# Last two layers of a four-layer stack: keys ahead of the weights' product on POOL, squares ahead of the turned weights on DVE

## The reference

```python
def _layer(x, wqkv, qs, ksc, wo, lg, lb, w1, b1, w2, b2):
    h = shift_token(x)
    q, k, v = split(h @ wqkv)              # 8 heads of 64
    q = l2norm(q) * qs;  k = l2norm(k) * ksc
    q, k = rotary_xpos(q, k)
    o = local_attention(q, k, v)           # softmax over this window of 64 and the one before
    x = x + o @ wo
    ...                                    # layer norm, gated feed-forward
    return x
```

## Time and profile before

| what | us |
|---|---|
| median of 3 runs | 1707.55 (1704.67 to 1719.86) |
| the profiled execution | 1716.1 |
| its span, first to last instruction | 1714.3 |
| PE busy (share of the span) | 1424.1 (83%) |
| DVE busy | 1084.5 (63%) |
| ACT busy | 780.0 (45%) |
| POOL busy | 401.3 (23%) |

### The profile page before, as it was taken

How to read it: one execution, slowest core, us unless ns; L and a number is a source line. 1 busy time by engine, 2 the same in 40 slices (tenths; PEclk the granted TensorE clock), 3 DMA queues, 4 the chain that set the end, 5 groups by cost and what they waited for, 6 DMA issues and landing times.

```text
span 1714.3 us, 25564 instructions
## 1 busy us (share of the span) xinstructions
PE 1424.1 (83%) x9075; PEld 819.3 (48%) x9075; DVE 1084.5 (63%) x2293; ACT 780.0 (45%) x1648; POOL 401.3 (23%) x258
## 2 busy tenths in 40 slices
PE   6999999999999689954579999984588868788766
PEld 4777777777777433222013333222255543355542
DVE  6776766766767537675646666514767744677644
ACT  2444544544444133322035656553367743477731
POOL 2000000000000103342202130001478830578811
PEclk9999999999999789976569999888689988699978
DMA  5000000000000000012201111102000000000000
GB/s 124 1 1 1 0 0 0 0 0 0 0 0 0 1 1 0 0 49 99 75 36 60 66 65 65 57 2 56 1 1 0 1 1 1 1 0 0 1 1 25
DMA packets 26097, 33.82 MB, mean 20 GB/s; under 512 B 5970, under 2 KB 20508, under 8 KB 24732
## 3 DMA queue, kind: packets, MB, share of 16 engines
q1 hardware_dynamic: 26028, 32.91, 6.0%
HBM read 28.51 MB, written 4.39 MB: 19 GB/s over the span
## 4 chain that ended last, share of the span: by engine, by line
PE 62%; POOL 14%; DVE 8%; issue 7%; ACT 3%; DMA 3%; SPq 2%; POOLq 0%; DVEq 0%; ACTq 0%
PE ps L658 14%; PE ps L689 7%; PE ps L700 7%; POOL d_rn L1954 5%; PE ps L894 5%; PE ps L914 5%; PE ps L872 4%; POOL probsT L1965 4%; PE ps L823 2%; POOL k_st L1952 2%; POOL q_st L1952 2%; PE ps L817 2%; PE ps L645 2%; PE ps L810 2%; DVE stats L1120 1%
## 5 line engine op out<-in xcount | busy, mean ns | idle before, releaser
L1731 ACT ACTIVATE probsT<-ps 128x512 f32<-128x512 f32 (+1 forms) x304 | 166.2, 575 | 153.8 <-PE ps L898 137.1
L1221 DVE TENSOR_REDUCE negmax<-ps 128x1 f32<-128x1024 f32 x128 | 150.7, 1219 | 76.1 <-PE ps L689 76.1
L1631 ACT ACTIVATE probs<-ps,negmax 128x1024 f32<-128x1024 f32 x128 | 142.7, 1115 | 76.2 <-DVE negmax L1221 75.9
L1637 ACT COPY probsT<-ps 128x512 f32<-128x512 f32 x128 | 75.0, 586 | 177.8 <-PE ps L700 177.7
L894 PE MATMUL ps<-arena 79*128 79x512 bf16 (+3 forms) x384 | 116.9, 350 | 31.1 <-DMA arena<-c_maxima 23.4
L700 PEld LDWEIGHTS ps<-ident,probs 128*128 128x128 f32 x1024 | 114.7, 141 | 58.3 <-issue 53.5
L1389 DVE CUSTOM_DVE_ANT_0 xn<-ps,arena 128x128 f32<-128x128 f32 (+7 forms) x128 | 93.3, 756 | 77.6 <-PE ps L872 76.1
L700 PE MATMUL ps<-ident,probs 128*128 128x128 f32 x1024 | 136.3, 276 | 0.0
L658 PE MATMUL ps<-probsT,v_nat 128*128 128x256 f32 x554 | 129.9, 380 | 0.0
L1389 DVE CUSTOM_DVE_ANT_0 xn<-ps,probs 128x128 f32<-128x128 f32 (+7 forms) x128 | 93.5, 756 | 56.8 <-PE ps L872 55.7
L689 PE MATMUL ps<-k_st,q_st 64*128 64x512 f32 x512 | 127.2, 615 | 2.2 <-DVE v_st L1200 1.4
(11 more groups left out here) (255 smaller groups left out, 2743.2 us busy)
## 6 DMA issues: line engine op xcount, KB each, us to landing
arena<-c_parts SPq DMA_DIRECT2D x32, 192.0 KB
c_parts<-probsT SPq DMA_DIRECT2D x4, 768.0 KB, 4.4
yT<-c_parts SPq DMA_DIRECT2D x32, 96.0 KB
arena<-c_parts SPq DMA_DIRECT2D x16, 128.0 KB
arena<-in_L_ffn_w_dram SPq DMA_DIRECT2D x3, 512.0 KB
work<-in_L_ffn_wqkv_dram SPq DMA_DIRECT2D x1, 1536.0 KB
q_st<-c_parts SPq DMA_DIRECT2D x16, 96.0 KB
k_st<-c_parts SPq DMA_DIRECT2D x16, 96.0 KB
```

Source lines behind the costliest of these rows:

```text
L1221: dve.tensor_reduce(negmax[:, u:u + 1], s2, AX_X, ALU.max, negate=True)\
L1631: act.activation(probs[:, u % NPB, :], s2, ACT.Exp, bias=negmax[:, u:u + 1], accum_out=rowsum[:, u:u + 1]).then_inc(s_a_exp, 1)
L1731: act.activation(c_p[:, kt % 2, j0:j0 + heads, q0 - kt * P:q0 - kt * P + n], ps[:, 4 + c % 2, 0:heads * n].rearrange("p (h n) -> p h n", n ...
```

## The change

POOL does `unit_norm` of tile t+2 ahead of the weights' product of tile t. The power then no longer stands behind the exponentials of tile t, so two things guard `d_rn`: DVE copies the queries' half of it to a new tile `d_rq`, from which the exponentials take their scale, and POOL's power waits for DVE's row product of tile t (`s_d_nm8`), which stands behind that copy. On DVE, `norms` of tile t+2 moves ahead of the copy of the turned weights of tile t-1.

```diff
--- before.py
+++ after.py
@@ -269,6 +269,7 @@
         d_nm = sb("d_nm", [P, 2, H2])
         d_nm8 = sb("d_nm8", [P, 2, H2])
         d_rn = sb("d_rn", [P, 2, 2 * H2])
+        d_rq = sb("d_rq", [P, 2, H2])
         d_sum = sb("d_sum", [P, 2, H2])
         d_rr = sb("d_rr", [P, 2, H2])
         d_mA = probs[:, 0:2, :]
@@ -1513,17 +1514,18 @@
                         dve.wait_ge(s_d_s, n + 1)
                         dve.tensor_reduce(d_nm[:, par, :], ps[:, 6:8, :].rearrange("p n (h c) -> p (n h) c", c=P),
                                           AX_X, ALU.max).then_inc(s_d_nm, 1)
+                        dve.tensor_copy(d_rq[:, par, :], d_rn[:, par, 0:H2])
                         dve.wait_ge(s_d_nm, n + 1)
                         dve.scalar_tensor_tensor(out=d_nm8[:, par, :].rearrange("p (c m) -> p c m", c=2),
                                                  in0=d_nm[:, par, :].rearrange("p (c m) -> p c m", c=2), scalar=-1.0,
                                                  in1=d_rn[:, par, 0:H2].rearrange("p (m c) -> p c m", c=2),
                                                  op0=ALU.mult, op1=ALU.mult).then_inc(s_d_nm8, 1)
+                    if exists(t, 2):
+                        norms(t + 2, par)
                     if exists(t, -1):
                         dve.wait_ge(s_d_pt, n)
                         dve.tensor_copy(d_pT[:, 4:8, :].rearrange("p h c -> p (h c)"), ps[:, 5, :])\
                            .then_inc(s_d_pT, 1)
-                    if exists(t, 2):
-                        norms(t + 2, par)
                     if exists(t, -2):
 
                         dve.wait_ge(s_d_w, n - 1)
@@ -1799,7 +1801,7 @@
                             hd = 2 * (h % 4) + h // 4
                             ins = act.activation(d_p[:, par, h, :], ps[:, 6 + h // 4, (h % 4) * P:(h % 4 + 1) * P],
                                                  ACT.Exp, bias=d_nm8[:, par, h:h + 1],
-                                                 scale=d_rn[:, par, hd:hd + 1],
+                                                 scale=d_rq[:, par, hd:hd + 1],
                                                  accum_out=d_sum[:, par, h:h + 1])
                         ins.then_inc(s_d_e, 1)
                     if exists(t, -1):
@@ -1951,6 +1953,8 @@
                     pool.wait_ge(s_d_m, n + 1)
                     pool.tensor_tensor(kq, d_mA[:, par, :], d_mB[:, par, :], ALU.add).then_inc(s_d_add, 1)
                     pool.wait_ge(s_d_cl, n + 1)
+                    if exists(t, -2):
+                        pool.wait_ge(s_d_nm8, n - 1)
                     pool.tensor_tensor(d_rn[:, par, :], ss[:, par, :], half_c[:, :], ALU.pow).then_inc(s_d_rn, 1)
                     pool.wait_ge(s_d_add, n + 1)
                     pool.wait_ge(s_d_rn, n + 1)
@@ -1959,13 +1963,13 @@
                         .then_inc(s_d_kq, 1)
 
                 def step(t, par):
+                    if exists(t, 2):
+                        unit_norm(t + 2, par)
                     if exists(t, 0):
                         v = d_p[:, par, :, :]
                         pool.wait_ge(s_d_rr, T0 + t + 1)
                         pool.tensor_tensor(v, v, d_rr[:, par, :].unsqueeze(2).to_broadcast([P, H2, P]), ALU.mult)\
                             .then_inc(s_d_p, 1)
-                    if exists(t, 2):
-                        unit_norm(t + 2, par)
 
                 unit_norm(0, 0)
                 unit_norm(1, 1)
```

## The result

The changed kernel takes 1796.09 us as a median of 4 runs (1794.47 to 1809.08), beside 1710.10 (1704.67 to 1719.86, 4 runs) for the kernel before: slower, ratio 1.0513 with a 95% interval of 1.0443 to 1.0583, +86.0 us. Its profiled execution took 1796.78, with a span of 1795.0. A ratio is estimated from the fast runs on the same chip, so it need not be the quotient of the two medians.

A forecast was written before the change was run, and what follows sets the result against it. A loop of waits, not an engine, was taken to set the pace: 9.62 + 1.38 + 1.22 = 12.22, with 1.7 for the clock 13.92 us per tile; with the ends +85.6, median 1793 us, range 1735 to 1820.

The forecast's parts named there:

- those of +108: Rival: the clock falls at the larger price, 2.61 us, in every tile; 14.83 us per tile, 1815 us; chance 0.07.
- The ring: Loop of waits from DVE's turned-weights copy through PE, ACT and DVE's rotation back to that copy: 9.62 us per tile.
- the wait: DVE's copy to d_rq, ahead of the row product, has to wait for POOL's add of the keys: +1.22 us per tile.
- the squares: DVE's sum (1.21) and clamp (0.17) now stand ahead of the copy of the turned weights: +1.38 us per tile.
- the clock: PE idles 3.9 us before line 1059, its clock falls, transposes and projection slow: +1.7 us in every tile.
- the loop through the exponentials: ACT's own loop: 9.93 + 1.22 = 11.15 us per tile, staying below the 12.22 us sum.
- the upper bound: For DVE's copy to d_rq beside POOL's add: bounds 0 and 1.22 us per tile, of which 1.22 was taken.
- the smaller of the two prices: Slowing of PE's transposes and projection (2.68 us) seen in the warm-up: +1.67 us, against +2.61.
- The rival in which the clock holds: PE's clock does not fall in the steady steps: 12.22 us per tile, +45 us, 1752 us; chance 0.17.
- the ends: Each layer's end: last-keys wait goes (2.2 us), last weights come 2.7 later, +0.5 us; step 0 counted separately at 1.22.
- The one that let nobody wait: Neither DVE's copy nor its row product waits for POOL: 11.00 us per tile, 1721 us, or 1762; chance 0.10.
- The rival on the other side: POOL's keys decide if the turned-weights copy (line 1523) ends before PE finishes line 1045: 1695 us; chance 0.06.

The follow-up runs named there:

- Experiment 1: Changed kernel with PE's output product of line 1046 computed four times over into the same place: 1769.24 us, ratio 1.0352.
- experiment 2: Changed kernel with DVE's sum and clamp put back behind the copy of the turned weights: 1730.44 us, ratio 1.0120.
- experiments 4 and 5: Both against the changed kernel: without the copy to d_rq, power waiting for the exponentials, 1802.21 us; POOL's row-product wait moved from power to add, 1793.92 us.
- experiment 3: Kernel before with only DVE's sum and clamp moved ahead of the copy of the turned weights: 1741.46 us, ratio 1.0195.
- Experiment 6: Changed kernel with POOL's row-product wait moved up to the add, and sum and clamp back behind the turned weights: 1717.84 us, ratio 1.0016.
- experiment 7: Kernel before with PE's projection of tile t+2 ahead of tile t's transposes, ACT and DVE reordered to suit: 1695.45 us, ratio 0.9925.
- experiment 8: Kernel before with PE's projection first, plus DVE's copy of value rows moved behind its copy of inputs: 1694.29 us, ratio 0.9888.

## Why the prediction was right

It gave 1793 us, +85.6; measured were 1796.09, +86.0. Its steps by the rows above, in us from a rotation, predicted and then measured: row product 4.80 and 4.78; line 1059 (now 1060) 7.06 and 6.97; the weights' product done 12.6 and 12.4; PE's idle time 3.9 and 3.80; the copy 1.3 and 1.40, ending with the add; transposes 1.9 and 1.97; clock below 0.9 and 0.87. No transposes waited for POOL, and the clamp released POOL's power. Two of the prediction's sums are off by rounding, without effect: the terms of 7.06 add up to 7.05, and those of +108 to +107.

**The loop.** The ring that the prediction put at 9.62 now reads: rotation to maximum 2.34 as before; maximum to row product 2.44 in place of 1.24; to the copy of the turned weights 1.41 in place of 0.09; copy and the start behind it 0.78, as before; line 1060 to the transposes 1.37 in place of 1.17; transposes to projection 1.76 in place of 0.90; projection to rotation 3.58 in place of 3.10. That is 13.68. The first two growths, 1.20 and 1.32, are the wait and the squares (predicted 1.22 and 1.38); the last three, 0.20 + 0.86 + 0.48 = 1.54, are the clock. Experiment 1, which gives back the clock alone, agrees: 12.10 (predicted 12.22) and 1.59 (predicted 1.7). So all three terms were a little too large, and a tile came to 13.68 in place of 13.92: 12 tiles took 164.18 and 163.22 us, not 167.0. That the loop through the exponentials is the next longest, with 11.15, had no row of its own in the prediction; experiment 2, with 11.13, bears it out.

**The copy's wait.** The value taken, the upper bound, was right, and experiments 4 and 5 show why it made no difference which operation waits: the row product or the clamp would have waited nearly as long.

**The clock.** That it would fall in every tile was the riskiest step, and it fell at a little under the smaller of the two prices (projection 2.39, not 2.68). Across the kernels here, with 1.76 us of idling before the weighted values it held in the steady steps of experiment 2 (1.00 from 1271.44 to 1371.42), with 2.7 to 2.8 in experiment 3 it fell in about every second tile, and with 3.8 in the changed kernel in each. The idle time ahead of that one line does not decide alone, since in the warm-up it fell with less. The rival in which the clock holds was wrong only in this; experiment 1 has its step, 12.10 us for 12.22, though not its 1752 us, since the added products lengthen the ends. The one that let nobody wait fell with the copy's 1.40.

**The term that was mis-sized** is the ends. The layer's end was put at +0.5 and measured 37.03 in place of 34.65 and 37.19 in place of 35.19, +2.4 and +2.0; step 0 was put at +1.22 and measured +1.29 and +1.95 (11.33 in place of 10.04 and 9.38). The clock had been charged to the 12 steady steps only. Behind the last rotation of layer 0, PE's timeline of the kernel after shows

```profile
1410.72 1.38 PE L1060 MATMUL ps<-probsT 128*64 128x64 f32 x32 [3.68 <-issue]
1412.04 1.97 PE L995 MATMUL ps<-ident,q_st 128*128 128x128 f32 x8
1413.80 1.59 PE L1007 MATMUL ps<-arena 128*128 128x512 f32 x2
```

where the kernel before had

```profile
1371.60 1.17 PE L1059 MATMUL ps<-probsT 128*64 128x64 f32 x32 [1.27 <-issue]
1373.63 1.09 PE L994 MATMUL ps<-ident,q_st 128*128 128x128 f32 x8 [0.86 <-POOL q_st L1958]
1374.56 1.02 PE L1006 MATMUL ps<-arena 128*128 128x512 f32 x2
```

0.21 + 0.88 + 0.57 = 1.66 us more in these three, which with the 0.5 is about what the ends lost. In layer 1 step 0's projection took 3.78 in place of 3.01, so 0.77 of its 1.95 is the clock too. The errors partly cancel: steps 1 to 13 cost 75.5 in place of 82.2, ends and steps 0 together 7.6 in place of 3.4. The sum of 83.1 stands beside a difference of the spans of 80.7; 2.1 of the rest is there before the first step, as the walk's first rotation came at 1212.60 in place of 1214.70.

That the medians differ by 86.0 us, 0.4 from the forecast, is luck: the traces confirm the working to about 3 us (83.1 for 85.6), with two errors of 6.7 and 4.2 that go opposite ways, the medians of the kernel before ranged from 1707.55 to 1717.03 over the comparisons, and the executions of one kernel lie 15 us apart and more.

**The rival on the other side** (the keys decide, 1695 us) was wrong about its point of decision, as the prediction said. Experiment 6 prices its core: with POOL's waits for the reciprocal gone and DVE's order restored, the step is 10.03 us in place of 10.25 (the rival's own figure was 9.93), and the time cannot be told from before. Experiments 7 and 8 are the other test of the loop: they leave POOL's order alone, shorten the ring that was named, and are faster.

What stays open: why the clock fell in about every second tile of experiment 3 and not in the ones between, with idle times alike (2.83 and 2.67 us). No run here varies the work between the gaps by itself.

## What to carry to other kernels

An engine that waits long is not yet an engine that anybody waits for: write out the ring of releases between two like instructions, in us, and charge each edit to it; here the removal of 10.6 us of POOL's waiting in six steps did not show in the time, and moving the projection by one place on PE, with what follows from it on ACT and DVE, was worth 0.75 to 1.1%. When the ring gets shorter, a wait that had been hidden can come onto it (experiment 7). When work is added to such a ring, add a second price if PE sits idle in it: here its clock fell and slowed the matmuls that followed, at the layer's ends as well as in the steady steps. Before POOL's large operation is moved, look for the small operations of DVE that will stand beside it.

## What was not expected of the hardware

**POOL's power does not hold DVE up, while its add and its products do.** Beside the add a copy of 8 columns took 1.40 us in place of 0.16, the clamp 1.29 in place of 0.17, the row product 1.28 in place of 0.15, each ending 0.03 behind the add; beside the weights' product the copy of 64x512 took 1.93 in place of 0.42 (experiment 7). Inside the power of 2.91 us, DVE's scalar copies of 128x128 took 0.21 and 0.22 (the rows of DVE and POOL of the kernel after), no more than with no POOL operation beside them (0.23 at 1342.92 in the kernel before), and that of 64x512 took 0.42 (experiment 8). The row product of the kernel before, which reads two tiles in SBUF, took its 0.17 at 1340.54 inside this one:

```profile
1338.48 2.91 POOL L1954 TENSOR_TENSOR d_rn<-ss,half_c 128x16 f32<-128x16 f32 x1
```

A reduction over 1024 columns ran beside the add in 1.22 (at 1337.89 in the kernel after), and took 1.21 behind it (1340.41). The Trainium skill ("SBUF — State Buffer", section "SBUF: two separate sides") says that whichever of the two engines starts first holds the shared port pair for the whole instruction and the other fully blocks, which goes for DVE's operations in a two-port mode and, beside a GpSimd operation that reads SBUF, for those with two SBUF inputs. The adds agree, the power doesn't, and here the measurement decides: by that rule the row product would have ended behind the power's end at 1341.39, and not at 1340.71. Why the power differs is not shown.

**More work can be faster.** Three repeats of the output product per tile, 2.7 us of PE's time, made the changed kernel 27 us faster: PE's transposes behind them took 1.08 us again, as at 2.4 GHz, in place of 1.97. It is no cure: 1769.24 us is still slower than the kernel before.
